# Decoder layer on one core: exact cross and self attention scores as plain fp32 products on 32 rows instead of split fp32r products on 64

## The reference

```
x = layernorm(x + linear_attention(x))            # 16 heads of 64, relu features
q, k, v    = heads(x Wq + bq), heads(x Wk + bk), heads(x Wv + bv)      # 16 heads of 16
y  = softmax(causal(q k^T / 4)) v
qc, kc, vc = heads(x Wcq + bcq), heads(ctx Wck + bck), heads(ctx Wcv + bcv)
y += softmax(qc kc^T / 4) vc                      # 512 queries, 1024 keys
x = layernorm(x + y Wp + bp)
x = layernorm(x + expert_of(argmax(gate(x)))(x))  # 8 experts, 256 -> 1024 -> 256
```

## Time and profile before

| | |
|---|---|
| median of 3 runs | 2286.91 us (2286.52 to 2288.45) |
| the profiled execution | 2287.69 us, span 2286.0 us |
| busy: PE, DVE, ACT, POOL | 2169.5 (95%), 1366.7 (60%), 1102.2 (48%), 367.5 us (16%) |
| mean granted TensorE clock | 0.994 of full speed |
| ACT exponentials (`L1201`) | 704, 665.3 us busy |
| DVE maxima of context scores (`L1412`) | 1024, 636.7 us busy |

### The profile page before, as it was taken

How to read it: one execution, slowest core, us unless ns; L and a number is a source line. 1 busy time by engine, 2 the same in 40 slices (tenths; PEclk the granted TensorE clock), 3 DMA queues, 4 the chain that set the end, 5 groups by cost and what they waited for, 6 DMA issues and landing times. The chain is left out here.

```text
span 2286.0 us, 51067 instructions
## 1 busy us (share of the span) xinstructions
PE 2169.5 (95%) x16290; PEld 1352.2 (59%) x16291; DVE 1366.7 (60%) x3905; ACT 1102.2 (48%) x1680; POOL 367.5 (16%) x628
## 2 busy tenths in 40 slices
PE   8999999999899999999999999999999899799998
PEld 4555554556455555555555645554555455499997
DVE  2588357844785458635883478357844685255554
ACT  1267524761477227732674257524762377233332
POOL 1011111111111111111111111111111111122222
PEclk9999999999999999999999999999999999899999
DMA  7440025102520162005300350026102520655553
GB/s 235 155 164 25 2 106 200 48 2 85 198 71 2 47 234 73 2 11 189 130 25 9 141 180 25 1 97 209 48 2 85 198 71 2 221 181 182 183 182 109
DMA packets 115763, 235.75 MB, mean 103 GB/s; under 512 B 19614, under 2 KB 42655, under 8 KB 113344
## 3 DMA queue, kind: packets, MB, share of 16 engines
q1 hardware_dynamic: 112112, 224.23, 29.3%
q0 software_dynamic: 3408, 8.41, 1.0%
HBM read 154.04 MB, written 73.17 MB: 99 GB/s over the span
## 5 line engine op out<-in xcount | busy, mean ns | idle before, releaser
L1201 ACT ACTIVATE es<-ps 128x1024 f32<-128x1024 f32 (+1 forms) x704 | 665.3, 984 | 250.7 <-PE ps L809 181.4
L1412 DVE TENSOR_REDUCE craw<-ps 128x1 f32<-128x512 f32 x1024 | 636.7, 684 | 115.0 <-PE ps L773 115.0
L773 PE MATMUL ps<-hk,hq 64*128 64x512 f32 x1024 | 391.4, 450 | 24.7 <-DVE craw L1412 8.6
L807 PE MATMUL ps<-hq,hk 64*128 64x512 f32 x1024 | 325.0, 440 | 2.2 <-ACT es L1201 2.2
L1408 DVE CUSTOM_DVE_ANT_0 ps<-ps,causal 128x512 f32<-128x512 f32 (+3 forms) x512 | 236.2, 518 | 91.4 <-PE ps L770 91.0
L773 PEld LDWEIGHTS ps<-hk,hq 64*128 64x128 f32 x1024 | 174.7, 184 | 194.8 <-DVE craw L1412 129.3
L809 PE MATMUL ps<-mrow,minus 64*128 64x512 f32 x1024 | 285.8, 391 | 0.0
L837 PE MATMUL ps<-es,vca 128*17 128x256 f32 x4096 | 276.6, 382 | 1.2 <-ACT es L1201 0.3
L661 POOL TENSOR_SCALAR_AFFINE_SELECT es<-es 128x256 f32<-128x256 f32 x256 | 99.0, 406 | 659.5 <-ACT es L1201 659.4
L1731 ACT ACTIVATE hT<-ph,b1s 128x128 f32<-128x128 f32 x312 | 89.2, 369 | 182.8 <-PE ph L1694 182.8
L809 PEld LDWEIGHTS ps<-mrow,minus 64*128 64x128 f32 x1024 | 166.0, 186 | 10.1
(11 more groups left out here) (210 smaller groups left out, 2838.3 us busy)
## 6 DMA issues: line engine op xcount, KB each, us to landing
w1s<-in_w1T SPq DMA_DIRECT2D x39, 1024.0 KB, 5.4
hk<-scr_kc SPq DMA_DIRECT2D x64, 512.0 KB, 5.1
scr_kc<-staged SPq DMA_DIRECT2D x16, 1024.0 KB, 4.3
scr_qc<-staged SPq DMA_DIRECT2D x32, 512.0 KB, 4.5
scr_q<-staged SPq DMA_DIRECT2D x32, 512.0 KB, 5.3
hq<-scr_qc SPq DMA_DIRECT2D x56, 256.0 KB, 4.4
hq<-scr_q SPq DMA_DIRECT2D x56, 256.0 KB, 4.2
hk<-scr_k SPq DMA_DIRECT2D x56, 256.0 KB, 4.6
```

The source lines that it names most:

```text
L773: last = mm(pb, hq[i][at, T + t * P:T + (t + 1) * P], hk[i][at, T + half * BANK:T + (half + 1) * BANK], start=True, stop=True)
L807: mm(pb[a], hk[i][rows[a], T + j * P:T + (j + 1) * P], hq[i][rows[a], T:2 * T], start=True, stop=False)
L1201: nc.scalar.activation(es[:, k % ERING, :].rearrange("p (a c) -> p a c", a=HB)[:, :, 0:w], eslot[k % 2][:].rearrange("p (a c) -> p a c", a ...
L1412: last = v.reduce_max(craw[p % 2][:, t, a:a + 1, 1 + half], pb, AX.X)
```

## The change

The products of `max_unit` and `exp_scores` become plain fp32. A head takes 32 rows: its 16 dimensions on the even rows. On the odd rows the keys hold -1 (set once) and the queries 0, except that row 1 of the query operand holds the maximum of each query, so that one product gives scores less maxima. Rows 0 to 63 hold the two heads for the exponentials, rows 64 to 127 the same two heads without maxima, for `max_unit`. The splitting, the scratch tensors and the block of minus ones go; staged queries and keys are loaded from SBUF to SBUF. The maxima are transposed as 16 rows, copied by one ACT instruction, and put into `hq` by two small loads a pair (`place_maxima`). There are four slots instead of five. A cycle takes its four units of maxima as two after each step, not one, two and one, and steps 0 to 3 take three each. The ring keeps its three banks.

```diff
-HROW = 4 * XD
-MROW = HROW // NT
+ROWS = 2 * XD
+MAXROW = 1
+MCOLS = 2 * 2 * NT
-("kc0", "B", ..), ("kc1", "B", ..), ("qc0", "B", ..), ("q0", "B", ..), ("k0", "B", ..)
+("kc0", "A", ..), ("kc1", "A", ..), ("qc0", "D", ..), ("q0", "A", ..), ("k0", "D", ..)
-SLOTS = 5
+SLOTS = 4
+LEAD = SLOTS - 1
-ROW_AFTER = (4, 6)
+MORE_FIRST = 4
+ROW_AFTER = 4
+FIRST_ROW = 2
...
-               ("qf0", 0, 4), ("qf0", 1, 4), ("qf1", 0, 4), ("qf1", 1, 4)]
+               ("qf0", 0, 4), ("qf0", 1, 4), ("qf1", 0, 4), ("qf1", 1, 3)]
...
-        order += take(1)
-        if k < steps:
-            order.append(("exp", *divmod(k, NU)))
-        order += take(HB)
-        if k + 1 < steps:
-            order.append(("exp", *divmod(k + 1, NU)))
-        order += take(1)
+        if turns and order[-1][0] == "weigh":
+            order.append(turns.pop())
+        for n in (k, k + 1):
+            if n < steps:
+                order.append(("exp", *divmod(n, NU)))
+            order += take(HB + (n < MORE_FIRST))
...
+            def load(name, p, to, col, done):
+                of, first = stage[name], p % (PAIRS // 2) * HB * XD
+                w = of.shape[-1]
+                for u in range(2):
+                    sp.dma_start(to[p % SLOTS][u * HB * ROWS:(u + 1) * HB * ROWS:2, col:col + w],
+                                 of[first:first + HB * XD, p // (PAIRS // 2), :]).then_inc(done[p % SLOTS], 16)
+            def place_maxima(b, p):
+                sp.wait_ge(s_turned, cur(b, PAIRS, p + 1))
+                sp.sem_inc(s_pace, 1)
+                for a in range(HB):
+                    at = a * ROWS + MAXROW
+                    sp.dma_start(hq[p % SLOTS][at:at + 1, :].rearrange("p (n c) -> p n c", c=P),
+                                 mrow[p % 2][a * 2 * NT:(a + 1) * 2 * NT, :]).then_inc(s_mrow, 16)
...
+                for p in range(PAIRS):
+                    place_maxima(b, p)
+                    if 1 <= p < PAIRS - LEAD:
+                        if p == 1:
+                            staged(b, "kc1", "qc1", "q1", "k1")
+                        sp.wait_ge(s_sc, cur(b, NEXP, p * NU))
+                        sp.sem_inc(s_pace, 1)
+                        load_cross_keys(p + LEAD)
+                        load_cross_queries(p + LEAD)
+                        load_own_queries(p + LEAD)
+                        load_own_keys(p + LEAD)
...
+            for i in range(SLOTS):
+                nc.gpsimd.memset(hk[i][:], -1.0)
+                nc.gpsimd.memset(hq[i][:], 0.0).then_inc(s_minus, 1)
...
-                pb, at = ring_slot(b, ("max", p, m)), slice(a * HROW, (a + 1) * HROW)
+                pb, first = ring_slot(b, ("max", p, m)), (HB + a) * ROWS
+                at = slice(first, first + ROWS)
...
-                    for a in turned:
-                        mm(pb[a], hk[i][rows[a], T + j * P:T + (j + 1) * P], hq[i][rows[a], T:2 * T], start=True, stop=False)
-                    for a in turned:
-                        last = mm(pb[a], neg[a], mrow[p % 2][rows[a], :], start=False, stop=True)
+                rows = [slice(a * ROWS, (a + 1) * ROWS) for a in range(HB)]
+                for j, col in (EXP_SELF[n] if n < NSELF else [(n - NSELF, 0)]):
+                    key, query, w = (j * P, j * P, T - j * P) if n < NSELF else (T + j * P, T, T)
+                    for a in range(HB):
+                        last = mm(pb[a][:, col:col + w], hk[i][rows[a], key:key + P], hq[i][rows[a], query:query + w],
+                                  start=True, stop=True)
...
-                    for t in range(NT):
-                        last = nc.scalar.activation(mrow[p % 2][:, t * P:(t + 1) * P], mbank[n % MBANKS][:, 0:P],
-                                                    ACT.Copy, scale=inblock[:, t:t + 1])
-                    last.then_inc(s_mrow, 1)
+                    nc.scalar.activation(mrow[p % 2][:], mbank[n % MBANKS][0:MCOLS, 0:P], ACT.Copy).then_inc(s_turned, 1)
```

More of the change, by code:

```diff
@@ L68 @@
 HALF = {"x1a": 0, "x1b": 1, "qc1": 0, "q1": 1, "proj0": 0, "proj1": 1}
-ACT_AT = {name: sum(who in "AB" for _, who, _, _ in JOBS[:n + 1]) for name, n in JN.items()}
-DVE_AT = {name: sum(who in "DB" for _, who, _, _ in JOBS[:n + 1]) for name, n in JN.items()}
+ACT_AT = {name: sum(who == "A" for _, who, _, _ in JOBS[:n + 1]) for name, n in JN.items()}
+DVE_AT = {name: sum(who == "D" for _, who, _, _ in JOBS[:n + 1]) for name, n in JN.items()}
 N_ACT, N_DVE = ACT_AT["kf3"], DVE_AT["kf3"]
[L74 to L78, removed]
+STAGED = ("kc0", "kc1", "qc0", "q0", "k0", "qc1", "q1", "k1")
 HB = 2
 PAIRS = XH // HB
-SLOTS = 5
-EARLY = 2
+SLOTS = 4
+LEAD = SLOTS - 1
 BANK = 512
[L86 to L90, removed]
+LOAD = 2 * 16
+LANDED = {p: 2 * LOAD * (p // SLOTS + 1) for p in range(PAIRS)}
+EACH = 2 * LOAD * (PAIRS // SLOTS)
 MAX_SELF = [[(3, 0)], [(2, 0), (0, 384)], [(1, 0)]]
@@ L146, in heads_order @@
     for k in range(0, steps + BEHIND, 2):
[L147 to L150, removed]
+        weighed = [m for m in (k - BEHIND, k - BEHIND + 1) if m >= 0]
         for m in weighed:
@@ L320, in attentions @@
         x1 = sb("x1", [P, NT, CR])
[L321 to L327, removed]
+        x1T = sb("x1T", [P, KC, T])
+        craw = [sb(f"craw{i}", [P, NT, HB, 2]) for i in range(2)]
         zk = sb("zk", [P, 2, T // 2])
@@ L497, in _ @@
                 sp.dma_start(xs_flat[:, n * BLANKS * CR:(n + 1) * BLANKS * CR], blank).then_inc(s_blank, 16)
[L499 to L505, removed]
-                        row = 2 * n + dup if name[0] == "k" else 2 * dup + n
-                        sp.dma_start(to[row:P:4, col:col + T].bitcast(F32), stage[0:HB * XD, stg, n, at:at + T].bitcast(F32)).then_inc(done, 16)
@@ L1168, in _ @@
                                          ACT.Copy).then_inc(s_act, 1)
-                high_part("kc1", 1, 1, TC_)
+                stage_part("kc1", 1)
                 nc.scalar.activation(x1T[:, 0, :], full("x1a"), ACT.Copy).then_inc(s_act, 1)
-                high_part("qc0", 3, 0, T)
-                high_part("q0", 2, 0, T)
-                high_part("k0", 0, 0, T)
-                def whole_part(name, bias_n):
-                    t = full(name)
-                    high_part(name, bias_n, 1, T, last=False)
-                    nc.scalar.activation(whole[:, POOL_LOW.index(name), :], t[:, 0:T], ACT.Identity,
-                                         bias=bias_c[:, bias_n, 1:2]).then_inc(s_act, 1)
+                stage_part("q0", 2)
                 def values():
@@ L1390, in _, with columns, own_col @@
                 layer_norm()
[L1392 removed]
                 v.tensor_copy(x1T[:, 1, :], full("x1b")).then_inc(s_dve, 1)
[L1394 to L1396 removed]
+                stage_part("qc0", 3)
+                stage_part("k0", 0)
+                def columns(p):
+                    return mpad[p % 2][:].rearrange("p (a w t) -> p a w t", a=HB, w=2)
+                def own_col(p, a, t):
+                    return columns(p)[:, a, 0, t:t + 1]
                 def reduce(p, m):
@@ L1401, in reduce @@
                     n, a = divmod(m, HB)
+                    if (n, a) == (2 * NT, 0) and p >= 2:
+                        dve.wait_ge(s_ring, cur(b, NRING, RING_AT["row", p - 2, 0] + 1))
+                        dve.sem_inc(s_held, 1)
                     dve.wait_ge(s_ring, cur(b, NRING, s + 1))
```

229 lines of the change are left out of this document (59 added, 170 removed), and 6 rows, old and new, of the table JOBS.

## The result

The changed kernel takes 2834.64 us (median of 4, 2828.5 to 2843.51) against 2287.57 (2286.52 to 2288.45): a ratio of 1.2395, 95% interval 1.2359 to 1.243. The forecast was 2708 with a range of 2560 to 2850. The time lies in the stated range, but outside the forecast's own 2640 to 2790. The profiled execution took 2831.86 us. The last line is the third group's counterpart on the page of before.

What follows compares the result with a forecast made beforehand. PE was taken as the bound, DVE 0.3 us behind. Staging -0.6, lead-in +7.7, middle +37.0 and tail +8.5 make 52.6 us a batch, times 8 = 421, on 2287.7: 2708 us, range 2560 to 2850 (own range 2640 to 2790).

Steps and rivals of the forecast that it cites:

- The price of a product: Score and maxima products: plain fp32 on 32 rows costs two records, 0.86 us for 512 columns, instead of 0.235.
- Rivals B (one record): Score and maxima products: one on 32 rows costs one record, 0.43 us; 2396 us in all, chance 0.08.
- C (0.235): Score and maxima products: one costs what fp32r does, 0.235 us; faster, 2268 us in all, chance 0.05.
- Fourfold overlap: Score and maxima products: four groups of 32 rows, two heads' scores and two heads' maxima, run together.
- rival A: Row groups overlap less than fourfold: 3030 us if twofold, 2835 us with rounds 1.3 times longer; chance 0.13.
- The loop through the ring: Cycle of two steps: with three banks, m4 waits for m1's reduction, making the cycle 3.96 us against 2.79.
- The middle: First exponential scores to last transposed maxima of a batch: from 109.7 to 146.7 us, plus 37.0.
- The lead-in: Batch part before the first exponential scores: from 27.2 to 34.9 us, plus 7.7.
- The tail at full clock: Last row of maxima to last kept result of a batch: from 19.4 to 27.9 us, plus 8.5.
- a clock under 1.00: Sign to look for in the middle of a batch: it would add to everything; no size given.
- Start and staging: Staging before the first maxima: second parts, scratch tensors and their waits go, minus 0.6 us a batch.
- rival D: First scores of a pair wait for a late row of maxima: 2836 us in all, chance 0.04.

Runs made afterwards that it cites:

- experiment 2: Kernel before, with only the maxima's products made plain fp32, still on 64 rows, scores staying fp32r: 2679.93 us.
- experiment 3: Changed kernel with fp32r products in place of plain fp32 on the same 32 rows, scores losing precision: 2388.63 us.
- experiments 1 and 4: Changed kernel both times. 1: DVE reduces only 256 of 512 columns, 2761.94 us. 4: each step's weighing, scores and two maxima in turn, 2698.74 us.
- experiment 8: Changed kernel with the last row of maxima transposed one step later: 2732.27 us; with extra unread products filling the tail as well: 2725.39 us.
- experiment 7: Changed kernel with two more unread products in every step from step 72 on, on the idle row groups: 2761.25 us, ratio 1.2076.
- experiment 5: Kernel before, with only the change's order of a cycle (two maxima after each step): 2393.99 us, ratio 1.0468.
- experiment 6: Changed kernel with the old order of a cycle (one maxima, scores, two, scores, one): 2759.08 us.

## Why the prediction came out as it did

**The price of a product: right.** Two records at a pitch of 0.43 us on 32 rows, 0.86 a product, and 0.10 more where the first waits for its weights. Rivals B (one record) and C (0.235) are out. That this price carries the change is shown from both sides: put on the maxima alone, it costs 392 us (experiment 2), and taken from the changed kernel, it gives 446 back (experiment 3), even though the clock falls there.

**Fourfold overlap: right; rival A is out.** Four records start within 20 ns, the next four 0.53 us later (0.10 of it for the first weights), the third round 0.43 after the second. Rival A's 2835 us is the measured time by chance only. The Trainium skill gives 3.07 times for four row groups (TensorE: Matmul & The Clock Gate, Measured speedup vs the span model); an estimate by it makes a round 1.3 times longer, 0.56 us. The timeline doesn't agree: it has 0.43, as for one tile alone.

**The loop through the ring: right.** Last maxima 1.9 us after the first: 1.95, released by DVE. DVE idle for 1.4 us a cycle: 1.41. A cycle of 3.96: 4.01. That it is the loop and not PE's own work is shown by experiments 1 and 4: a shorter reduction and the same products gave 8.3 us a batch, another order of the same products 14.2. One reading of the prediction is doubtful, without harm to its sum: that PE bounds the kernel before. Its own block sum leaves 0.2 of the 2.79 us unexplained, its formula for the loop gives 2.71, and the weight loads waited 129.3 us for DVE; no run tested it.

**The middle: 4.1 us a batch too small** (+37.0 against +41.1, 33 us in all). Between the starts of the weighing blocks after, 11 cycles (two pairs) take 46.08 us. The prediction had 45.1 for them, with rows, results and a split. Plain cycles give 0.3 of the missing 1.0 (six at 4.00 to 4.01 for 3.96). The rest is in the other five: 5.23 us with a result, a row and a split weighing, 4.76 with a result, 4.39 with a row, 4.18 and 3.49 with own keys. All 33 cycles take 137.7 us for 135.2, the first ones, up to the first weighing, 8.8 for 8.3, and the cut-off one up to the last row 4.3 for 3.2. The last 1.1 goes with the 1.38 us for which PE waits for the last reductions, a wait that the prediction doesn't name.

**The lead-in: right** (+7.7; measured +7.6). Groups of three maxima stand there with 1.9 us, as costed.

**The tail at full clock: 1.2 us too large** (+8.5; +7.25). The cycle is the predicted 2.9 us (1236.68 to 1239.59); where the 1.2 went was not followed.

**The step that failed: the clock.** The tail was summed with every product at 2.4 GHz, and of a clock under 1.00 the prediction only said that it "would add to everything", in the middle, where it did not fall. It fell in the tails, and that is 94 us, with 8 in the lead-ins. The terms at full clock give 2287.7 + 442 = 2730 us, 22 from the forecast, within its own range. (The kernel without the wait measures 2732, with tails 1.1 us shorter and 10 us of falls in its lead-ins.) The fall in the tails hangs on the 1.38 us for which PE waits for the last maxima: cutting that wait is enough to keep the clock there (experiment 8). The work on half of the rows makes the fall long: with the rows filled it still comes, and ends sooner (experiment 7). Before has nearly the same wait, 1.29 to 1.31 us, and no fall in any of its eight tails; its products there stand on 64 rows. Whether that is the reason was not tried, and it is no full guard: with the new order (experiment 5) the wait is 1.42 us, and the clock falls in one tail of eight, for 3.4 us.

**Luck.** The time lies in the stated range because the upper end, 2850, was put there for half of rival A, which is out. A term that the prediction left at nothing used that room.

**The order** was not a term of its own, and should have been: the old one is 3.6 us a batch better in the changed kernel, and 12.9 in the one before.

**Start and staging** (-0.6; -0.7 worked out from the span), and **rival D** (the row of maxima late) as predicted. What PE and its weight loads waited for before the records of the scores, from the view of that line after (us, times):
```profile
  issue: 218.9, 684
  ACT es L1109: 33.2, 64
```
No load is among it, and the 64 waits for ACT lie at other steps than a pair's first, so the row of maxima is always there in time.

**Left open.** Two tails of eight have the same 1.38 us wait and the same matmuls, and no fall; in experiment 6 (1.00 us) six of eight. What decides was not found. Nor is it known why the clock falls in lead-ins without a wait, and in the middle of experiment 3, after waits of some 0.5 us. A fourth bank for the ring, which would break the loop, was not tried, since all eight banks of PSUM are in use.

## What to carry to other kernels

Price a product by its records and columns: here plain fp32 costs 0.86 us where fp32r costs 0.235, and four groups of rows in place of two did not earn that back. Where a ring of buffers is shorter than the units of a cycle, add up the loop through it (product, result, reduction, signal, product) before counting busy time; then it pays to let other work of the busy engine run beside the loop's waits. And before a stage with thin matmul work, look for the wait at its door: here one line that shortens a wait of 1.4 us to 0.5 is worth some 100 us, 94 of them through the clock.

## What the hardware showed that was not expected

- The clock fell to 1.2 GHz for 30.7 us (five times) and 47.8 us (once) in tails in which PE was busy without a break (40.90 of 40.90 us), after a wait of 1.38 us. With that wait cut to 0.52 us, it fell in none of eight, and with 1.00 us in two of eight.
- More matmul work was faster: 64 more matmul records in each tail made the kernel 73 us faster, because the clock's falls there got shorter.
- Four groups of 32 rows with 128 columns each overlap fully: four products in the time of one (0.43 us a record).
